# Graph attention on one core: the ends of a window are turned in another bank, the mish ratio lies in PSUM, and ScalarE's biases are immediate

## What is computed

```python
e_att  = x[src] @ Ws + bs + edges @ We + be          # per edge, 4 x 32
recv   = x[dst] @ Wr + br
logits = mish(e_att + recv) . attn_w + attn_b        # mish(z) = z * tanh(softplus(z)), one logit a head
w      = softmax of logits over the edges of a receiver
out    = sum over the edges of a receiver of w * e_att
y      = layernorm(x + out)
```

## Time and profile before

| | us |
|---|---|
| median of three runs | 2174.07 |
| lowest, highest | 2173.88, 2176.59 |
| span of the profiled execution | 2661.8 |
| ACT, PE, DVE, POOL busy in it | 1927.7, 1917.4, 1895.0, 1575.1 |

### The profile page before, as it was taken

One profiled execution on the slowest core, in us unless ns is written; L12 is line 12 of the kernel. 1 busy time (PEld: TensorE's weight loads), 2 busy tenths in 40 slices (PEclk: granted clock), 3 DMA queues, 4 the chain that ended last, 5 costly groups with the idle time before them and its releaser, 6 DMA issues.

```text
span 2661.8 us, 45397 instructions
## 1 busy us (share of the span) xinstructions
PE 1917.4 (72%) x13621; PEld 1789.2 (67%) x13621; DVE 1895.0 (71%) x3941; ACT 1927.7 (72%) x3126; POOL 1575.1 (59%) x1640
## 2 busy tenths in 40 slices
PE   5667777777776777776776777776777777776776
PEld 5567666766666776766666766666667676666665
DVE  2676777777777767776676777766777777677766
ACT  1777777777777777777777777777777777777774
POOL 2666656656666665666566656656666666556661
PEclk8888888888888887888888888878888888878877
DMA  6422322322232322232232232232223232223220
GB/s 191 130 77 80 105 83 78 112 79 77 81 111 77 97 96 77 77 113 79 76 112 79 78 105 86 78 100 90 78 93 99 79 98 95 77 86 104 79 79 17
DMA packets 106714, 240.18 MB, mean 90 GB/s; under 512 B 45800, under 2 KB 72546, under 8 KB 99658
## 3 DMA queue, kind: packets, MB, share of 16 engines
q1 hardware_dynamic: 53334, 132.54, 14.6%
q0 software_dynamic: 52224, 107.06, 14.1%
q10 hardware_dynamic: 1128, 0.25, 0.0%
HBM read 229.98 MB, written 9.74 MB: 90 GB/s over the span
## 4 chain that ended last, share of the span: by engine, by line
DVE 36%; PE 20%; another core or an unknown queue 18%; issue 17%; ACT 7%; DVEq 1%; DMA 1%; ACTq 0%; SPq 0%
PE ps_sum L827 7%; DVE Z L1122 6%; DVE tbuf L1138 6%; DVE tbuf L1129 6%; DVE Z L1205 5%; PE ps_z L815 4%; PE ps_z L816 4%; DVE onehot L1113 4%; DVE logit L1144 2%; PE ps_edgeT L793 2%; ACT tbuf L933 1%; ACT tbuf L930 1%; ACT tbuf L936 1%; ACT tbuf L923 1%
## 5 line engine op out<-in xcount | busy, mean ns | idle before, releaser
L717 POOL DMA_INDIRECT landing<-xs_table,src_i x1632 | 1574.2, 965 | 1034.1 <-issue 448.3
L815 PE MATMUL ps_z<-we_sb,edgeT 128*128 128x128 f32 x3264 | 767.2, 320 | 83.3 <-issue 82.4
L816 PE MATMUL ps_z<-xr_buf,onehotT 128*128 128x128 f32 x3264 | 751.9, 315 | 72.3 <-issue 71.5
L827 PE MATMUL ps_sum<-Z,onehot 128*128 128x132 f32 x3264 | 558.9, 321 | 204.7 <-DVE att L1224 95.2
L815 PEld LDWEIGHTS ps_z<-we_sb,edgeT 128*128 128x128 f32 x3264 | 613.0, 232 | 100.9 <-issue 97.3
L816 PEld LDWEIGHTS ps_z<-xr_buf,onehotT 128*128 128x128 f32 x3264 | 609.4, 231 | 83.1 <-issue 82.8
L827 PEld LDWEIGHTS ps_sum<-Z,onehot 128*128 128x128 f32 x3264 | 485.6, 224 | 223.8 <-issue 149.4
L1113 DVE TENSOR_TENSOR onehot<-iota_f,ps_dve 128x512 f32<-128x512 f32 x408 | 276.0, 677 | 432.5 <-remote 352.6
L923 ACT ACTIVATE tbuf<-Z,c_zmax 128x512 f32<-128x512 f32 x408 | 296.2, 726 | 165.7 <-DVE Z L1122 85.9
L907 ACT COPY edgeT<-ps_edgeT 128x512 f32<-128x512 f32 x408 | 235.3, 577 | 229.4 <-remote 179.9
L798 PE MATMUL ps_onehotT<-ident_half,onehot 128*128 128x128 bf16 x1632 | 176.6, 232 | 241.8 <-issue 103.8
(11 more groups left out here) (110 smaller groups left out, 1228.3 us busy)
## 6 DMA issues: line engine op xcount, KB each, us to landing
landing<-in_edge_attr_dram SPq DMA_DIRECT2D x51, 2048.0 KB
landing<-xs_table,src_i POOLq DMA_INDIRECT x1632
x_in<-in_x_dram SPq DMA_DIRECT2D x51, 64.0 KB
xr_in<-xr_table SPq DMA_DIRECT2D x51, 64.0 KB
out_dram<-y_out SPq DMA_DIRECT2D x51, 64.0 KB
xr_buf<-xr_table SPq DMA_DIRECT2D x50, 64.0 KB
xs_table<-onehot SPq DMA_DIRECT2D x2, 896.0 KB
xr_table<-landing SPq DMA_DIRECT2D x1, 1568.0 KB
```

The lines of the kernel that those rows point to most:

```text
L717: nc.gpsimd.indirect_dma_start(gath[b][:, t, :], None, xs_dram, bass.IndirectOffsetOnAxis(ap=src_i[:, b, t:t + 1], axis=0))\
L815: nc.tensor.matmul(ps_z[q][:, j, :], edgeT[:, q, j, :], we_sb[:, :], start=True, stop=False)
L816: mm = nc.tensor.matmul(ps_z[q][:, j, :], onehotT[:, q, j, :], xr_buf[:, b, :], start=False, stop=True)
L827: mm = nc.tensor.matmul(ps_sum[:, 0:ZC], OHv[:, b, t, :], Zv[:, b, t, :], start=(t == 0), stop=(t == T - 1))
```

## The change

It has four parts.

1. The turned one-hots of a group are packed as bf16 into the first 256 f32 columns of their bank, now called `ps_turned`. The other 256 columns of its first four partitions take two turned columns of ends: the keys (`far_ends`) ahead of the one-hots of the turn in group 1, the maxima (`row_max`) ahead of those in group 2. ACT copies them out just ahead of its copy of the one-hots (`items`, L941).
2. `ps_ends` is gone. What else it held moves into spare columns of `ps_dve` and `ps_sum`; the turned-back maxima go to columns of `ps_sum`, so the first sum of the next window waits until DVE has read them.
3. The bank that came free is `ps_ratio`: the last of the five activations writes there, and the multiply reads it from there (L1163) and still writes `tbuf`. It has one buffer, so the last activation of group g waits for the multiply of group g-1.
4. The biases of the five activations are immediate numbers; `c_zmax` is gone.

The core of the diff:

```diff
-        ps_onehotT = ps("ps_onehotT", [P, GT, P])
+        ps_turned = ps("ps_turned", [P, 512])
...
-        ps_ends = ps("ps_ends", [P, 512])
-        item_run = ps_ends[0:H, 2 * P:4 * P]
-        rcv = ps_ends[:, D:2 * D]
+        rcv = ps_dve[:, 2 * D + 2 * T:3 * D + 2 * T]
         run_max = rcv.rearrange("p (h t) -> p h t", t=T)
-        att2 = ps_ends[:, 2 * D:3 * D]
+        att2 = rcv
+        item_run = ps_dve[0:H, D + 2 * T:D + 2 * T + 2 * P]
+        back = ps_sum[:, 2 * P:2 * P + 2 * H]
+        ps_ratio = ps("ps_ratio", [P, GT, D])
+        def turned(q):
+            return ps_turned[:, 0:2 * P].bitcast(BF16).rearrange("p (t n) -> p t n", n=P)
+        def turned_ends(q):
+            return ps_turned[0:H, 2 * P:4 * P]
...
                 wait(pe, onehotT_ready, at(w, g) - 1)
+                if ends:
+                    ends(q)
                 for j in range(n):
-                    tr = nc.tensor.transpose(ps_onehotT[:, j, :].bitcast(BF16)[:, 0:P],
-                                             halves(OHv[:, b, a + j, :]), ident_half[:, :])
+                    tr = nc.tensor.transpose(turned(q)[:, j, :], halves(OHv[:, b, a + j, :]), ident_half[:, :])
...
                     wait(pe, fin, (w - 1) * FIN + FIN_READ)
+                    pe.wait_ge(seg, w * SEG + SEG_A + SEG_B + 2)
...
+            def far_to_row(w, b):
+                def ends(q):
+                    pe.wait_ge(prep, w * PREP + PREP)
+                    two_rows(q, (far_ends[:, b, 0, :], far_ends[:, b, 1, :]))
+                return ends
+            def maxima_to_row(w):
+                def ends(q):
+                    pe.wait_ge(seg, w * SEG + SEG_A)
+                    two_rows(q, (row_max[:, :, 0], row_max[:, :, T - 1]))
+                return ends
...
+            def copy_onehotT(w, b, g, ends=None):
                 n = GROUPS[g][1]
                 q = g % 2
                 act.wait_ge(onehotT_ps, at(w, g))
                 wait(act, z_ps, at(w, g) - 2)
+                if ends:
+                    items(q, ends)
+                nc.scalar.copy(onehotT[:, q, 0:n, :], turned(q)).then_inc(onehotT_ready, 1)
...
-                nc.scalar.activation(tb, Zv[:, b, a:a + n, 0:D], ACT.Relu, bias=c_zmax[:, 0:1], scale=-1.0)\
+                nc.scalar.activation(tb, Zv[:, b, a:a + n, 0:D], ACT.Relu, bias=ZMAX, scale=-1.0)\
...
-                    nc.scalar.activation(tb, tb, ACT.Square, bias=c_one[:, 0:1]).then_inc(sq_done, 1)
+                    nc.scalar.activation(tb, tb, ACT.Square, bias=1.0).then_inc(sq_done, 1)
...
                     act.wait_ge(ln_done, at(w, g))
-                    nc.scalar.activation(tb, tb, ACT.Exp, bias=c_ln2[:, 0:1], scale=-1.0).then_inc(ratio_ready, 1)
+                    wait(act, mish_ready, at(w, g) - 1)
+                    nc.scalar.activation(ps_ratio[:, :, :].rearrange("p t d -> p (t d)"), tb, ACT.Exp, bias=LN2,
+                                         scale=-1.0).then_inc(ratio_ready, 1)
...
-                nc.vector.scalar_tensor_tensor(out=tb, in0=tb, scalar=1.0, in1=Zv[:, b, a:a + n, 0:D],
+                nc.vector.scalar_tensor_tensor(out=tb, in0=ps_ratio[:, :, :], scalar=1.0, in1=Zv[:, b, a:a + n, 0:D],
                                                op0=ALU.subtract, op1=ALU.mult, reverse0=True)\
                     .then_inc(mish_ready, 1)
```

More of the change, by code:

```diff
@@ L55 @@
 NLATER = 3
-VCONST = 12
-IOTAS = 11
+VCONST = 11
 SEARCH = 3
@@ L776, in _ @@
             pe.wait_ge(s_base, 2)
-            nc.tensor.matmul(ps_ends[:, 0:W + 2], ones_row[:, :], base_row[:, :], start=True, stop=True)\
+            pe.wait_ge(s_first_xr, 1)
+            nc.tensor.matmul(ps_sum[:, 2 * P:2 * P + W + 2], ones_row[:, :], base_row[:, :], start=True, stop=True)\
                 .then_inc(s_base_ps, 1)
@@ L782, in count_unsorted, with turn @@
                 pe.wait_ge(base_ready, 1)
-                nc.tensor.matmul(ps_ends[0:1, 64:66], ones[0:GN, 0:1], counts[:, :], start=True, stop=True)\
+                nc.tensor.matmul(ps_sum[0:1, 2 * P:2 * P + 2], ones[0:GN, 0:1], counts[:, :], start=True, stop=True)\
                     .then_inc(s_count, 1)
-            def turn(w, b, k, g):
+            def turn(w, b, k, g, ends=None):
                 a, n = GROUPS[g]
+                q = g % 2
                 if g == 0:
@@ L829, in sums, with two_rows @@
                 mm.then_inc(sum_ready, 1)
[L831 to L836, removed]
+            def two_rows(q, pair):
+                for c, ends in enumerate(pair):
+                    nc.tensor.transpose(turned_ends(q)[:, c * P:(c + 1) * P], ends, ident[:, :])
+            def far_to_row(w, b):
[8 more added lines that the diff above has]
+                return ends
             def maxima_back(w):
@@ L841, in maxima_back, with last_ends @@
                 for c in range(2):
-                    tr = nc.tensor.transpose(ps_ends[:, c * H:(c + 1) * H], im[:, c, :], ident[0:H, 0:H])
+                    tr = nc.tensor.transpose(back[:, c * H:(c + 1) * H], im[:, c, :], ident[0:H, 0:H])
                 tr.then_inc(back_ps, 1)
+            def last_ends(ends, g):
+                if g == 2:
+                    pe.wait_ge(items_ready, 2 * W - 1)
+                ends(g % 2)
+                pe.drain().then_inc(onehotT_ps, 1)
             def window(w, b, k):
@@ L849, in window @@
                     w1, b1, g1 = two_after(w, b, g)
+                    ends = None
+                    if g == 1 and there(w - 1):
+                        ends = far_to_row(w - 1, 1 - b)
+                    if g == 2 and there(w - 1):
+                        ends = maxima_to_row(w - 1)
                     if there(w1) and there(w):
-                        turn(w1, b1, k if w1 is w else (k + b if b else k), g1)
+                        turn(w1, b1, k if w1 is w else (k + b if b else k), g1, ends)
+                    elif ends:
+                        last_ends(ends, g)
                     for m in SUM_LAST.get(g, []) if there(w - 2) else []:
@@ L963, in window @@
                     here, coming = there(w), there(w1) and there(w)
+                    ends = {1: item_far, 2: item_val}.get(g) if there(w - 1) else None
                     if coming:
                         copy_edgeT(w1, b1, g1)
-                        copy_onehotT(w1, b1, g1)
+                        copy_onehotT(w1, b1, g1, ends)
+                    elif ends:
+                        last_items(g, ends)
                     if here:
```

37 lines of the change are left out of this document (13 added, 24 removed).

## The result

The changed kernel takes **2125.12 us** (median of four runs, 2123.26 to 2126.94) where the kernel before takes 2174.73 (median of four): a ratio of 0.9766, 95% interval 0.9755 to 0.9778. It is 49.6 us faster; the forecast was 2137 us, 36.5 us faster by its own terms.

The account below looks back on a forecast made before the run. POOL was taken as the bound, its gathers 1.248 us apart, 39.9 us a window. 2174.1 less 35 (ratio in PSUM) and 1.5 (biases) gave 2137.6, forecast 2137 us, range 2090 to 2168.

Parts of the forecast that it names:

- Part 1: Ratio moved to PSUM for DVE's mish multiply: gathers stop waiting for it, 35 us gained, bounds 20 and 60.
- All three prices: Estimates of Part 1's gain: 33.6 us counted in the profile, 31.9 left over in the timed median, 42 scaled.
- The 31.9 us left over: Timed median 2174.07 us less 2142.2 for first gap, gathers at 1.248 us and tail; taken as gathers' delay.
- The factor of 1.24: Window of 50.2 us profiled against 40.6 timed; scaled the 33.6 us of gather delay to 42 us.
- Part 2: Immediate biases of ACT's five activations: 77 ns each, 157 us of ACT's time, nearly all becoming idle time.
- The 1.5 us at the end of the kernel: Part 2's gain behind the last gather: four groups of activations at 0.385 us each, bounds 0 to 3 us.
- The price for writing PSUM: ACT's last exponential writing PSUM: 0.1 us less to 0.1 us more each, nothing in the sum.
- Part 3: ACT's last exponential waits for DVE's multiply of the previous group, ratio having one bank: wait moved, cost 0.
- rival C: Slower: single ratio bank ties ACT to DVE, delaying copies, PE and gathers; 77 us, 2216 us; chance 0.08, 0.1 with other mishaps.
- Part 4: Rearranged transposes and copies of the ends on PE and ACT: maxima a third of a group later, nothing waits.
- A: ACT and DVE are the bound, not POOL; biases gain 50 to 100 us, middle 2095 us; chance 0.14.
- B: No change: gather delay hidden in waits for z, or another DVE operand contends; 2174 within 4 us; chance 0.12.

Follow-up runs that it names:

- b0_again: The kernel before, unchanged, run once more for a second profile: 2172.83 us.
- msg_sbuf_2: The changed kernel with the message multiply reading its weights from Z in SBUF instead of PSUM, on another chip than msg_sbuf: 2205.88 us, ratio 1.0157 to the kernel before.
- bias_only: The kernel before with the five activations' biases as immediate numbers and nothing else: 2178.59 us against 2174.88, ratio 1.0017.
- pointer_biases: The changed kernel with the biases of the five activations read from tiles again: 2126.83 us, ratio 0.9775 to the kernel before.
- after: The changed kernel with all its parts, in its first profiled measurement: median 2125.12 us, ratio 0.9766 to the kernel before.
- ratio_sbuf: The changed kernel with the ratio written to SBUF and read from there by the multiply, the rest kept: 2181.51 us, ratio 1.0028 to the kernel before.
- msg_sbuf: The changed kernel with the message multiply's weights read from Z in SBUF: 2614.65 us on a chip where the kernel before takes 2610.8.
- clean: The changed kernel with one input of the maxima's small DVE operations moved to PSUM: 2636.92 us against 2610.8 for the kernel before on that chip.
- half_before: The kernel before with only two of the four gathers of a group issued, so the output differs: 2063.53 us.
- half_after: The changed kernel with only two of the four gathers of a group issued, so the output differs: 2002.43 us.

## Why the prediction was right, and where its size was off

**The bound.** Right. POOL's step of 1.248 us stood in the lowest busy share of all engines, and the table above shows that nothing else carries the time.

**Part 1, the term that paid.** The mechanism was right, the size was not: 35 us predicted, 49.9 us of the gathers' time measured, inside the bounds of 20 and 60. All three prices lean on the profile of 2661.8 us, and the runs show what was wrong with each.
- The 33.6 us counted there are right for that execution (33.0 in 211 gathers), but the undisturbed kernel has 310 such gathers and 56.0 us.
- The 31.9 us left over took a first gap of 15.3 us and a tail of 51.8 us from it. With b0_again's own rows: 37.2 + 1631 x 1.248 + 37.9 = 2110.6, and 2172.8 - 2110.6 = 62.2 us are left, of which the gathers' excess is 58.9 and 1.9 lie outside the span. The sentence on the upper bound had named this case ("if the tail or the first gap are shorter in a timed run"); it was the true one.
- The factor of 1.24 for the closer packing was too small: 310 / 211 is 1.47, and the excess of each rose too, from 0.156 to 0.181 us (33.0 / 211 and 56.0 / 310). Why is argued, not shown: DVE's add follows the landing of gathers, so in an undisturbed run the multiply keeps its place in POOL's step, while stalls scatter it.

That two of the three prices agreed within 2 us was no support, since both leaned on the same disturbed execution. The "middle" of the three, 35, is loosely taken: their median is 33.6 and their mean 35.8. What it meant by a gather that waits for the multiply's end is right in kind; measured, the gather ends 0.82 us behind that end, so it loses the rest of the multiply less about 0.12 us (1.40 us in place of 0.94 with 0.58 us to run).

The Trainium skill's rule ("SBUF — State Buffer", Who interferes with whom) would have made this part 0. The runs contradict its inference that such an operation doesn't stall the making of descriptors, for gathers like these, with the multiply (56.0 us of excess before, 0.1 after) and with a plain two input operation on SBUF (msg_sbuf_2, 80.2 us). These gathers also read their indices (`src_i`) from SBUF; whether they are held there or where they write was not separated by any run.

**Part 2, the biases.** 77 ns each predicted; 722 - 630 = 92 ns measured, and ACT's busy time fell by 174.0 us in bias_only, where 157 was predicted. The Trainium skill's 93 ("ScalarE: Activation LUTs", What ACT_TABLE_LOAD costs) agrees with the 92 ns. That they are worth almost nothing here was right: bias_only gained nothing. The 1.5 us at the end of the kernel are neither confirmed nor refuted: behind the start of the last gather stand 37.9 us in b0_again and 37.6 in bias_only, but 40.0 in pointer_biases and 38.6 in after, each from one execution. The price for writing PSUM had been left within 0.1 us either way; it is 602 - 630 = 28 ns less.

**Part 3, the new wait.** Right, 0. L980 stands idle 12.9 us over 408 runs, exactly as L976, which has no such wait. The waits of 113.5 us and 83.5 us in the earlier trace rows on which rival C rested were the stalled execution's: in b0_again they are 0.6 and 4.0, in after 2.0 and 5.4. Rows of after, groups by form:

```profile
L985 ACT ACTIVATE Z<-shifted 128x128 f32<-128x128 f32 x51 | 21.6, 423 | 5.4 <-DVE shifted L1227 5.4
...
L1199 DVE TENSOR_TENSOR item_pen<-item_far 4x255 f32<-4x255 f32 x51 | 20.7, 406 | 0.0
...
L1213 DVE TENSOR_TENSOR ends_max<-pen_tail,ps_sum 128x128 f32<-128x128 f32 x51 | 13.7, 269 | 0.0
L1213 DVE TENSOR_TENSOR ends_max<-pen_head,ps_sum 128x128 f32<-128x128 f32 x51 | 13.6, 266 | 2.0 <-PE ps_sum L861 2.0
```

**Part 4, the ends.** Right, 0: L1199, which waits for the copied ends, stands idle 0.0 us, as the prediction's count of a third of a group had it.

**The rivals.** A fell with bias_only and the table. B, no change, fell with the result itself; ratio_sbuf shows that the gathers' waits cost time. C fell with the idle time of L980. (The middle of A's 50 to 100 us is 2099 us, not 2095.) That the granted clock of PE is 0.898 in after and 0.917 in b0_again cost nothing either: POOL waits for PE's z for 20.5 us in all in after and 20.4 in b0_again.

## What to carry to other kernels

Look for the engine with a steady step of its own before reading busy shares: the gathers were 74% busy and set the time, ACT was 88% busy and its 174 us less work brought nothing. Where GpSimd issues gathers all the time, give every larger DVE operation on two tensors one operand in PSUM; here that was worth 50 us, and 83 us the other way for one operation more on SBUF alone. And where a profile took much longer than the timed runs, take only durations of single instructions from it: counts of coincidences, gaps and tails are all those of another execution, and prices that lean on them don't confirm each other.

## What the runs showed of the hardware

- A gather that starts inside an operation of DVE with two SBUF inputs is held to that operation's end: the multiply, a plain multiply of tensors, and a scan on four partitions (1.40, 1.44, 1.32 us in place of 0.94). Of the delayed gathers 191 of 199 (b0_again) and 224 of 224 (msg_sbuf_2) end 0.81 to 0.83 us behind the operation's end; behind the scan L1202 of after all 15 end 0.74 to 0.76 us later. With one of the inputs in PSUM there is no wait, though the other input and the output lie in SBUF (0.1 us of excess over 211 gathers).
- An activation of 128x512 f32 that writes PSUM takes 602 ns, into SBUF 630; with a tile as bias 692 and 722.
- In the first profile of the kernel before, and on the chip of msg_sbuf and clean, PE stands still in the middle of a group again and again; on that chip the kernel before takes 2610.8 us in place of 2174. PE's timeline of msg_sbuf there:

```profile
751.58 0.27 PE L824 MATMUL ps_z<-xr_buf,onehotT 128*128 128x128 f32 x1
752.31 0.35 PE L824 MATMUL ps_z<-xr_buf,onehotT 128*128 128x128 f32 x1 [0.46 <-issue]
753.72 0.27 PE L823 MATMUL ps_z<-we_sb,edgeT 128*128 128x128 f32 x1 [1.06 <-issue]
754.43 0.27 PE L823 MATMUL ps_z<-we_sb,edgeT 128*128 128x128 f32 x1 [0.44 <-issue]
```

  Nothing that the profile shows ends these pauses. Of pauses over 0.5 us between two products of the same line the first profile of the kernel before has 145 and msg_sbuf 141, b0_again and after three each. On msg_sbuf's chip half_before and half_after, with half the gathers, had five and three. That suggests that the gathers have a part in it; how, and why there only, stays open. So does why clean, 4 us faster than the changed kernel elsewhere, was 1% slower than the kernel before there, since the changed kernel itself was not run on that chip.
